# Multi-query attention: the inverse softmax sums go through DRAM to reach all partitions

## The reference, cut to what matters

```python
q = (xn @ Wq).reshape(b, n, HEADS, DIM_HEAD).transpose(0, 2, 1, 3)
kv = xn @ Wkv
k, v = (kv[..., :DIM_HEAD], kv[..., DIM_HEAD:])
...
attn = jax.nn.softmax(sim, axis=-1)      # sim: scores + bias, causal, with the null key's column
out = attn @ v                           # then the output projection and a layer norm
```

## Time and profile before

| what | value |
|---|---|
| median of 3 runs | 3480.68 us (3479.48 to 3484.33) |
| the profiled execution | 3474.07 us |
| its span, first to last instruction | 3472.4 us |
| mean granted TensorE clock | 0.943 of full speed |
| first loop (`cond2_0`) | about 852.9 to 1317.5 us |
| second loop (`cond1`) | about 1818.6 to 2270.8 us |
| third loop (`cond2_1`) | about 2549.8 to 3009.6 us |

### The profile page before, as it was taken

How to read it: one execution, slowest core, us unless ns; L and a number is a source line. 1 busy time by engine, 2 the same in 40 slices (tenths; PEclk the granted TensorE clock), 3 DMA queues, 4 the chain that set the end, 5 groups by cost and what they waited for, 6 DMA issues and landing times. The chain is left out here.

```text
span 3472.4 us, 50397 instructions
## 1 busy us (share of the span) xinstructions
PE 3121.6 (90%) x17344; PEld 2114.4 (61%) x17346; DVE 1963.2 (57%) x4663; ACT 1565.1 (45%) x3744; POOL 290.9 (8%) x609
## 2 busy tenths in 40 slices
PE   7999799989999998846879999988899999969996
PEld 5555566554777777432237777775467777746664
DVE  3556455445776766865457777734467777542223
ACT  1110455534666661633336666623356666413332
POOL 0003000000111100000000000000011111002222
PEclk8998899999999999878979999999899999979998
DMA  1008344027444431010252222101653535331112
GB/s 38 18 14 169 42 51 51 2 84 220 139 134 137 133 96 37 1 29 1 79 171 68 80 68 80 42 19 34 190 162 121 154 119 156 119 135 36 34 34 88
DMA packets 208730, 293.70 MB, mean 85 GB/s; under 512 B 25357, under 2 KB 145421, under 8 KB 208352
## 3 DMA queue, kind: packets, MB, share of 16 engines
q1 hardware_dynamic: 204746, 280.38, 29.1%
q0 software_dynamic: 3744, 10.23, 0.9%
HBM read 222.00 MB, written 68.10 MB: 84 GB/s over the span
## 5 line engine op out<-in xcount | busy, mean ns | idle before, releaser
L1981 ACT ACTIVATE cond_p<-cond_p,cond_negm 128x128 f32<-128x128 f32 (+7 forms) x768 | 593.1, 775 | 414.3 <-DVE cond_negm L2012 413.5
L1962 PE MATMUL ps_o<-cond_pt,cond_v 128*64 128x256 f32 (+1 forms) x3840 | 479.3, 371 | 5.3 <-DVE attn_out L2048 0.5
L1940 PE MATMUL ps_s<-cond_k_high,cond_q_high 128*128 128x512 f32 (+3 forms) x1152 | 441.3, 389 | 10.3 <-DVE cond_negm L2012 7.5
L2012 DVE CUSTOM_DVE_ANT_0 cond_p<-ps_s,cond_side,cond_null_scores 128x128 f32<-128x128 f32 (+7 forms) x512 | 403.9, 812 | 30.7 <-PE ps_s L1942 24.7
L1942 PE MATMUL ps_s<-cond_k_both,cond_q_both 128*128 128x512 f32 (+3 forms) x1152 | 388.6, 350 | 0.0
L1952 PE MATMUL ps_t<-ident,cond_p 128*128 128x128 f32 x2304 | 349.6, 281 | 6.8 <-ACT cond_pt L1986 4.8
L1962 PEld LDWEIGHTS ps_o<-cond_pt,cond_v 128*64 128x64 f32 x3840 | 237.7, 136 | 168.3 <-issue 70.9
L1952 PEld LDWEIGHTS ps_t<-ident,cond_p 128*128 128x128 f32 x2304 | 250.4, 141 | 106.4 <-issue 77.5
L1179 ACT ACTIVATE attn_pt<-ps_t 128x512 f32<-128x512 f32 (+3 forms) x384 | 172.7, 490 | 251.0 <-PE ps_t L1140 196.4
L1940 PEld LDWEIGHTS ps_s<-cond_k_high,cond_q_high 128*128 128x128 f32 x1152 | 220.9, 192 | 43.6 <-DVE cond_negm L2012 20.4
L2020 DVE COPY cond_pt<-ps_t 128x512 f32<-128x512 f32 (+1 forms) x240 | 140.3, 585 | 167.5 <-PE ps_t L1952 165.8
(11 more groups left out here) (417 smaller groups left out, 4842.0 us busy)
## 6 DMA issues: line engine op xcount, KB each, us to landing
mqa_q_halves<-cond_q_cut SPq DMA_DIRECT2D x96, 512.0 KB, 6.2
cond_q_both<-mqa_q_halves SPq DMA_DIRECT2D x384, 128.0 KB, 3.3
cond_q_high<-mqa_q_halves SPq DMA_DIRECT2D x192, 128.0 KB, 3.0
cond_side<-in_fside_16xSxS SPq DMA_DIRECT2D x32, 512.0 KB, 6.9
moe_experts<-in_L_ffn_W SPq DMA_DIRECT2D x16, 1024.0 KB, 12.3
cond_side<-in_fside_16xSxS SPq DMA_DIRECT2D x32, 448.0 KB, 5.6
cond_side<-in_fside_16xSxS SPq DMA_DIRECT2D x32, 384.0 KB, 5.2
cond_side<-in_fside_16xSxS SPq DMA_DIRECT2D x32, 320.0 KB, 4.7
```

The lines of the kernel that those rows point to most:

```text
L1940: nc.tensor.matmul(m.S[k % 2][:, lo:hi], c32(a.Q1[i][:, h, s * P:(s + 1) * P]), c32(a.K1[:, keys]), start=True, stop=False)
L1962: last = nc.tensor.matmul(sums[u % ON][h * HD:(h + 1) * HD, s0 * P:2 * P], a.V[:, b * QB + kb, :], PT[c % PT_SLOTS][:, (2 * h + s0) * P:(h ...
L1981: nc.scalar.activation(p, p, ACT.Exp, bias=negm[u % SMALL][:, r:r + 1], scale=-1.0, accum_out=rsum[u % SMALL][:, r:r + 1]).then_inc(exped, 1)
L2012: nc.vector.tensor_tensor_reduce(out=probs(u, r, 0, q + 1), in0=m.S[k % 2][:, 0:L], in1=toep_back(u, h, L) if cosine else a.side[h][:, SID ...
```

## The change

The step `spread` is gone, with the GpSimd copy, the two transposes, the ACT copy, the buffer `RB` and the place that it took among the three banks. In its place SP does the following in each unit, at the place of `den` in the list of steps: it waits for the inverse, stores `rinv` (128 partitions x 4 numbers) to DRAM transposed, in pieces of 4 bytes, waits for that store to land, and issues two DMAs that read 256 numbers (1 KB) back to each of 64 partitions. `out` waits for both. SP's queue is no longer over the units but over the list of steps: `load_queries` and `load_side` stand where the unit's last row stands. There are four buffers `RS` in place of two, each with its own semaphores.

```diff
@@ mqa_order @@
         if c[1] == MQA_UNITS[c[0]][2] + 1:
-            if spreads and spreads[0][1] == c[0]:
-                steps.append(("spread", spreads.pop(0)[1]))
             steps.append(("out", c[0]))
...
-            if spreads and n_groups - spreads[0][0] >= 2:
-                steps.append(("spread", spreads.pop(0)[1]))
@@ stage_mqa_loop @@
-    slots = [s for s in steps if s[0] in ("turn", "spread")]
+    slots = [s for s in steps if s[0] == "turn"]
...
-    RS = [m.sb(f"{name}_rs{i}", [P, 2 * P], F32, m.XTAT + 2048 * PT_SLOTS + i * 1024) for i in range(2)]
-    RB = [m.sb(f"{name}_rb{i}", [P, 2, P], F32, m.XTAT + 2048 * PT_SLOTS + 2048 + i * 1024) for i in range(2)]
+    RS = [m.sb(f"{name}_rs{i}", [P, 2 * P], F32, m.XTAT + 2048 * PT_SLOTS + i * 1024) for i in range(SMALL)]
...
@@ sync @@
-            for u, (pair, b, q0) in enumerate(MQA_UNITS):
-                n = u % PAIR_UNITS
+            def spread_inverse(u):
+                i = u % SMALL
+                sp.wait_ge(inv, u + 1)
+                if u >= SMALL:
+                    sp.wait_ge(done, u - SMALL + 1)
+                sp.dma_start(d["mqa_inv"][i].rearrange("k p -> p k"), rinv[i], allow_slow_non_contiguous=True).then_inc(inv_stored[i], 16)
+                sp.wait_ge(inv_stored[i], 16 * (u // SMALL + 1))
+                for h in range(2):
+                    row = d["mqa_inv"][i, 2 * h:2 * h + 2, :].rearrange("s q -> (s q)").rearrange("(a n) -> a n", a=1)
+                    sp.dma_start(RS[i][h * HD:(h + 1) * HD, :], row.broadcast_to([HD, 2 * P])).then_inc(inv_in[i], 16)
+
+            for step in steps:
+                if step[0] == "den":
+                    spread_inverse(step[1])
+                if step[0] != "row" or step[2] != 3:
+                    continue
+                u = step[1]
+                pair, n = divmod(u, PAIR_UNITS)
                 sp.wait_ge(added, 4 * (u + 1))
                 if u + Q_SLOTS < U:
                     a.load_queries(sp, u + Q_SLOTS)
...
@@ gpsimd @@
-                if step[0] == "den":
-                    u = step[1]
-                    pool.wait_ge(inv, u + 1)
-                    if u >= 2:
-                        pool.wait_ge(spread, u - 1)
-                    nc.gpsimd.tensor_copy(RB[u % 2][:, :, :].rearrange("p s (h w) -> p s h w", h=2),
-                                          rinv[u % SMALL][:, :].rearrange("p (h s) -> p s h", s=2).unsqueeze(3)
-                                          .broadcast_to([P, 2, 2, HD])).then_inc(wide, 1)
@@ tensor @@
-                elif step[0] == "spread":
-                    u = step[1]
-                    out = slot_free(pe, step)
-                    pe.wait_ge(wide, u + 1)
-                    for s in range(2):
-                        last = nc.tensor.transpose(out[:, s * P:(s + 1) * P], RB[u % 2][:, s, :], m.ident[:, :])
-                    last.then_inc(spread, 1)
@@ scalar @@
-                elif step[0] == "spread":
-                    u = step[1]
-                    act.wait_ge(spread, u + 1)
-                    if u >= 2:
-                        act.wait_ge(done, u - 1)
-                    nc.scalar.copy(RS[u % 2][:, :], slot_bank(step)[:, 0:2 * P]).then_inc(spread_sb, 1)
@@ vector @@
                     if u >= SMALL:
-                        dve.wait_ge(wide, u - SMALL + 1)
+                        dve.wait_ge(inv_stored[u % SMALL], 16 * (u // SMALL))
...
-                    dve.wait_ge(spread_sb, u + 1)
+                    dve.wait_ge(inv_in[u % SMALL], 32 * (u // SMALL + 1))
```

More of the change, by code:

```diff
@@ L1294, in mqa_order @@
     rows = [(u, r) for u in range(len(MQA_UNITS)) for r in range(4)]
-    steps, spreads, waiting = [], [], []
-    ahead, finished, chunk, n_groups = 0, -1, 0, 0
+    steps, waiting = [], []
+    ahead, finished, chunk = 0, -1, 0
     def place(limit, most):
@@ L1328, in mqa_order @@
                 steps.append(("den", u))
-                spreads.append((n_groups, u))
             if g == q0:
@@ L1337, in mqa_order @@
             place(ROWS_AHEAD, len(rows))
-            n_groups += 1
     for c in waiting:
@@ L1827, in stage_mqa_loop @@
     negm, rsum, nulla, nulle, dn, rinv = ([t[:, i, :] for i in range(SMALL)] for t in small)
-    qk, added, exped, turned, by_act, by_dve, attended, null_arg, null_exp, den, inv, wide, spread, spread_sb, done = (
+    qk, added, exped, turned, by_act, by_dve, attended, null_arg, null_exp, den, inv, done = (
         m.sem(f"{name}_{s}") for s in ("qk", "added", "exped", "turned", "copied_act", "copied_dve", "attended", "null_arg",
-                                       "null_exp", "den", "inv", "inv_wide", "spread", "spread_sb", "done"))
+                                       "null_exp", "den", "inv", "done"))
+    inv_stored = [m.sem(f"{name}_inv_stored{i}") for i in range(SMALL)]
+    inv_in = [m.sem(f"{name}_inv_in{i}") for i in range(SMALL)]
     side_masked = [m.sem(f"{name}_side_masked{g}") for g in range(4)]
@@ L1853, in slot_free @@
         k = slot_of[step] - TN
-        if k >= 0 and slots[k][0] == "turn":
+        if k >= 0:
             copied(pe, slots[k][3])
-        elif k >= 0:
-            pe.wait_ge(spread_sb, slots[k][1] + 1)
         return turns[slot_of[step] % TN]
@@ L2045, in _ @@
                     dve.wait_ge(attended, last_chunk[u])
-                    dve.wait_ge(spread_sb, u + 1)
+                    dve.wait_ge(inv_in[u % SMALL], 32 * (u // SMALL + 1))
                     tokens = b * S + q0 * P
-                    nc.vector.tensor_tensor(m.OT[:, pair, tokens:tokens + 2 * P], sums[u % ON][:, 0:2 * P], RS[u % 2][:, :],
+                    nc.vector.tensor_tensor(m.OT[:, pair, tokens:tokens + 2 * P], sums[u % ON][:, 0:2 * P], RS[u % SMALL][:, :],
                                             ALU.mult).then_inc(done, 1)
@@ L3051, in scratch @@
     d["mqa_q"] = nc.dram_tensor("mqa_q_halves", [2, HEADS * HD, B * S], F32, kind="Internal").ap()
+    d["mqa_inv"] = nc.dram_tensor("mqa_inverse_sums", [SMALL, 4, P], F32, kind="Internal").ap()
     d["distance"] = nc.dram_tensor("distance_bias", [HEADS, S + P], F32, kind="Internal").ap()
```

## The result

The changed kernel takes 4738.83 us (median of 4 runs, 4729.02 to 4748.09) beside 3480.08 us for the kernel before on the same chip (3473.44 to 3484.33, 4 runs). The forecast of 3492 us and its range up to 3535 us were far too low.

What follows compares the result with a forecast made beforehand. PE was taken to bound all three loops. A gain of 69.0 us against losses of 54.6 (stalls), 13.6 (clock), 8 (queue) and 4 (loop ends) summed to +11.2 us: 3492 us, range 3420 to 3535.

Steps and rivals of the forecast that it cites:

- The new chain: SP's path from inverse to loaded factors: store 2.2 us, issue 0.6, loads 2.7, hand-overs 0.2, in all 5.7 us.
- deadline of 7.4 us: In units with q0 = 0, `out` must start within 7.4 us of the inverse; every us beyond stops PE.
- Rival (b): 4-byte pieces are dear: a store of 4.2 us makes short units late, about +90 us and 3580 us; chance 0.18.
- unit 20: Units with q0 = 0, b = 1, first and third loop: store behind bias DMAs, 14 stalls of 3.9 us, 54.6 us.
- rival (a): Bias DMAs don't hold up the store; only SP's issuing delays such units, stall 0.6 us: -57, 3424 us; chance 0.24.
- The gain on PE: PE in all loops loses 192 spreads of 0.22 us (42.2 us) and waits; 69.0 us gained in all.
- terms of 14.8 and 3.4 us: PE's nine waits for GpSimd's widening copy (14.8 us) and two half-clock stretches after them (3.4 us) would go.
- the 8.6: In 48 units with q0 = 0, PE's 0.18 us wait for `out`, held by ACT's copy, would go: 8.6 us.
- The loops' ends: Output weights, issued behind each loop's last chain, land late and delay PE's first product with them: 4 us loss.
- 13.6 of clock: After 8 of the 14 long PE stalls the clock halves, losing 1.7 us each: 13.6 us, bounds 0 and 23.8.
- 8 for the queue behind the largest bias DMAs: SP, held by stores around the 1920 KB bias, is free late for the next q0 = 0 unit: 14 x 0.6 us.
- Rival (c): Nothing to be seen: stalls and gain cancel, or PE waits for DVE instead; -5 to +5 us; chance 0.06.

Runs made afterwards that it cites:

- 16-byte kernel: Changed kernel with its store in 128 pieces of 16 bytes instead of 512 of 4 (factors in another order): 3532.49 us, ratio 1.0142.

## Why the prediction was wrong, point by point

**The step that failed** is in "The new chain": "The 2 KB store is nearest to 2.0 by size and has half as many pieces as that load, so I take 2.2 us." It is 9.7 us, beyond the upper bound of 6.2 as well. The rows chosen to price it were the nearest by bytes and by number of pieces, but none was a write of small pieces that lie side by side in DRAM, which could be read off the address pattern. The 12-byte pieces lie side by side too, but they were a load; that such a read is cheap rests on this one DMA. With the pieces 512 bytes apart the guess would nearly have held (2.6 us).

**What that did to the rest.** The chain was treated as a delay to be held against a deadline of 7.4 us. At 9.7 us another limit comes first: SP handles one chain at a time. Store, wait, loads and queries together are 12.8 us, where a unit took 7.07. Rival (b) had the mechanism, dear pieces, with a chance of 0.18, but priced them at 4.2 us and counted stalls against the deadline, which gave 3580 us. The point where SP's sum for a unit passes PE's was never worked out. PE without the spreads needs 434.9 / 64 = 6.8 us per unit, SP needs the store's time and 1.2 + 1.9 + 0.2 = 3.3 us, so in the second loop the point is a store of 3.5 us. The loop with pieces 16 bytes apart fits: a mean of 4.5 us from store to loads makes 7.8 us per unit, and 512.6 / 64 = 8.0 were measured. A slip in the sum of rival (b): the 14 units behind the largest bias DMAs are in its 34 and in its 28. The "second" before the landing, in the prediction's part on unit 20 and in rival (a), is a microsecond.

**Behind the store.** "Whatever SP issues behind bias DMAs comes after them" was right and applies to the store itself. That its own slow landing would delay the queries and loads behind it was not seen. SP without the wait still takes 415 us more than the kernel before.

**The gain on PE** was right. The 16-byte kernel's second loop, with its store on time, is 17.3 us shorter; 64 x 0.22 + 16 x 0.18 are 17.0. The deadline of 7.4 us is confirmed too. Over the 48 units with q0 = 0 of the 16-byte kernel, PE doesn't wait where `out` starts up to 7.3 us after the inverse; it waits 0.07 us at 7.6, 3.9 at 11.4 and 7.3 at 14.8, so one us for each beyond 7.5. The terms of 14.8 and 3.4 us together, and the 8.6 by itself, were tried as above. The loops' ends, forecast at 4 us, are 3.3 there: the first product with the output weights starts 8.8, 9.6 and 9.5 us after the last inverse, where it was 8.2 each time.

**The bias loops** were under-sized even with a quick store. For the 14 late units the prediction gave 54.6 us of stall, 13.6 of clock and 8 for the queue behind the largest bias DMAs. In the 16-byte kernel PE's idle time in the two loops exceeds the second loop's by 45.3 + 43.2 = 88.5 us, and its busy time, at a granted clock of 0.94 and 0.95, by 20.5 + 14.9 = 35.4 us: 124 us where 76 were forecast. The chain in unit 20 is 14.7 us from inverse to `out`, not 11.3 (timelines of DVE and PE, the 16-byte kernel's first loop):

```profile
1009.94 0.18 DVE L2026 RECIPROCAL cond_rinv<-cond_dn 128x4 f32<-128x4 f32 x1
...
1024.83 0.42 DVE L2036 TENSOR_TENSOR attn_out<-ps_o,cond_rs 128x256 f32<-128x256 f32 x1 [8.20 <-DMA cond_rs<-mqa_inverse_sums]
...
1025.40 1.98 PE L1963 MATMUL ps_o<-cond_pt,cond_v 128*64 128x256 f32 x8 [7.22 <-DVE attn_out L2036]
```

SP is 4.5 us late, not 2.3, because it comes from the chain of the unit before and only then issues two units' queries and eight bias DMAs. Over the 14 such units SP is 3.8 us late on average and `out` comes after 13.2 us. The store itself, forecast at 5.6 us there (7.9 - 2.3), takes 6.0. `out` holds PE up 24 times, not 14. So with the store's price right the forecast would still have been some 40 us low, and the sign would have been right.

**Rival (a)**, a store that bias DMAs don't hold up, is refuted: 6.7 us behind them, and 7.4 us even with them on another queue. **Rival (c)** is out with the size of the effect.

## What to carry to other kernels

Before a small DMA is priced by its bytes, look at the addresses it writes: pieces of 4 bytes side by side landed after 9.7 us here, the same bytes as 16-byte pieces or far apart after 2.4 to 2.6. When a queue is made to wait for a landing, add up all that the queue does in one round and hold it against the round's length, besides the deadline of the single step. Moving one mask and one pair of transposes by a step brought 36 us, where the replacement of the whole path lost 1259.

## What the hardware showed that was not expected

- The landing of a store of 512 pieces of 4 bytes goes with their density in DRAM: 9.7, 8.0, 4.4, 3.0 and 2.6 us at 4, 8, 16, 32 and 512 bytes apart. Half as many at 4 bytes apart take 9.0, and 128 pieces of 16 bytes at 16 bytes apart 2.4.
- Independent DMAs behind such a store land nearly as late as it does (10.3 us): queries at 8.5 and 9.0 us in place of 3.0 and 3.3 in the kernel before, the 64 KB loads at 9.8 in place of 2.7 in the kernel with the pieces 512 bytes apart.
- A 2 KB store takes 7.5 us in the median of 14 units though the bias DMAs around it are on another queue.
- In the changed kernel, where PE waits for up to 24 us, its mean granted clock over a loop is 0.77 to 0.79, in place of 0.99 to 1.00. It is busy for 1565.5 us in the loops' windows where it was 1347.5, with fewer instructions. No run shows that these 218 us cost time: SP's sum alone makes up a unit's 12.85 us. Behind the 7.2 us wait of the 16-byte kernel's unit 20, eight products take 1.98 us at a granted clock of 0.50; in its second loop, without a wait before them, they take 1.08.
